# Queries rotated by VectorE from the raw projection, values projected in the odd slots, in a six-layer windowed transformer stage

## The chip, the cores and the metric

The kernel runs on one core of one Trainium2 chip, as one launch. The metric is the device time of that launch in microseconds. A program of many stages runs one after the other on the core's five engines: TensorE (matrix products and transposes), VectorE, ScalarE, GpSimd and SyncE, which only issues DMAs here.

## The reference, cut to what matters

The model is a chain of attention and feed-forward blocks on a tensor of 4 x 512 tokens with 128 features. The change is in one of them, `L2_ffn`, a transformer of six layers with 16 heads of 64 features and a window of 32 tokens:

```python
def attn_layer(x, Wqkv, qs, ksc, Wo):
    q, k, v = jnp.split(x @ Wqkv, 3, -1)          # heads of 64
    q = l2norm(q) * qs                            # q / max(|q|, 1e-12)
    k = l2norm(k) * ksc
    q = q * cos * scale + rotate_half(q) * sin * scale
    k = k * cos * inv + rotate_half(k) * sin * inv     # inv = 1 / scale
    out = local_attention(q, k, v)                # window 32, this block and the one before
    return out.transpose(0, 2, 1, 3).reshape(b, n, INNER) @ Wo

def ffn_layer(x, g, bln, W1, b1, W2, b2):
    hg = (layernorm(x) * g + bln) @ W1 + b1        # 2 x 341 columns
    a, gate = jnp.split(hg, 2, -1)
    return a * gelu(gate) @ W2 + b2

for i in range(6):
    x = attn_layer(shift_tokens(x), ...) + x
    x = ffn_layer(shift_tokens(x), ...) + x
```

The norm is one number for each token and head, so it can be multiplied in before or after the rotation.

## The kernel before

The stage is `transformer32` (line 780). The tokens are cut into 16 tiles of 128; the 16 heads into two groups of 8. A layer has thus 32 groups, and the six layers have 192, numbered n or G. The work is written by hand as a software pipeline over **slots**, one for each group (`slots()`): in slot s, group s is `now` (scores, softmax, weighing of the values), s+1 is `turn` (its rotated queries and keys are transposed), s+2 is `mid` (its keys are rotated), s+3 is `ahead` (projected, squared, summed, normalised, its queries rotated). A tile is finished every second slot. In even slots TensorE also mixes the heads of a tile (`mix_heads`) and makes the second feed-forward product of the tile before (`down`); in odd slots it makes the layer norm's transposes (`turn_sum`, `turn_norm`) and the first feed-forward product (`gate_up`), and ScalarE the Gelu, which wants another function table and back again (lines 1247 and 1253). An even and an odd slot together, a pair, are one tile of one layer.

Each engine does its part of every slot in a fixed written order and waits on semaphores for the others. What touches the change:

- `project` (line 1043, matmul on 1055) makes queries, keys and values of a group, each 128x512, into three PSUM banks `wa`. Before, all three of `ahead` are made in each slot. The values are copied into SBUF by ScalarE (`copy_v`, 1244), from where SyncE moves pieces of them by DMA into `vw` (`move`).
- ScalarE squares queries and keys (`square`, 1205); VectorE sums them by head (`sums`, 1299), limits them from below (`floor`, 1303); ScalarE makes inverse roots with a logarithm and an exponential (`roots`, 1217 and 1219); VectorE multiplies them into queries and keys (`normalise`, 1310), giving `qn`.
- GpSimd rotates (`rotate`): a product with the cosines into `ra` (999), two half-wide products with the sines into `rb` (1000, 1001), and their sum (1010 for keys, 1016 for queries).
- TensorE transposes the result (`turn_qk`, 1093), the softmax's numerators (`turn_p`, 1085) and the weighed output (`turn_o`, 1112). VectorE's `t_o` (1372) is the weighed output divided by its sums, and `t_ln` (1366) the normalised tile of the feed-forward part.
- VectorE's order in a slot: `add_heads` (1319, odd), scores' maximum and difference (1345, 1347), `gated` (1326, even), layer norm's statistics (odd), the queries' sums, `add_ffn` (1334, even), the keys' sums, the floor, `t_ln` (odd), `t_o`, and `normalise` of queries and keys.
- Of the feed-forward part's 341 columns the third chunk has 85, and its instructions work on 85 rows or columns (`HC`).

Of the kernel before, what the change touches and what calls it, by code (L numbers as in the profile page):

```python
# [20 lines left out]
P = 128  # L21
# [758 lines left out]
def transformer32(nc, g, dram, name, depth, heads, hid, wqkv, qs, ks, wo, ln_g, ln_b, w1, b1, w2, b2):  # L780
# [32 lines left out]

    wa_job, T_job, T_list = {}, {}, []
# [8 lines left out]

    with Stage(nc, name) as st:
        w_qkv = st.sb("w_qkv", [P, 2, 3 * INNER])
        w_o = st.sb("w_o", [P, 2, heads // 2, DIM])
        w_1 = st.sb("w_1", [P, 2, 2 * hid])
# [15 lines left out]
        ssq = st.sb("ssq", [P, 2, 16])  # L843
        logs = st.sb("logs", [P, 2, 16])
        inv = st.sb("inv", [P, 2, 16])
        qn = st.sb("qn", [P, 2, 8, HD])
# [30 lines left out]
        zeroed = st.sem("zeroed")  # L877
        resid_in = st.sem("resid_in")
# [13 lines left out]
        normed = st.event("normed", 2)  # L892
        q_rot = st.event("q_rot", 3)
        k_rot = st.event("k_rot", 3)
        q_roped = st.event("q_roped")
        k_roped = st.event("k_roped")
# [33 lines left out]
        with nc.Block() as block:  # L930
            @block.sync
            def _(sp):
                def load(l):
# [10 lines left out]
                    sp.dma_start(w_1[:, z, :], w1[l]).then_inc(sem, 16)  # L944
# [13 lines left out]

                load(0)
                sp.wait_ge(zeroed, 4)  # L960
# [25 lines left out]
            def _(pool):  # L986
                pool.memset(vn[:, :, :, :, :], 1.0).then_inc(zeroed, 1)
# [4 lines left out]
                def rotate(kind, n):  # L992
                    r, done = (0, q_rot) if kind == "q" else (1, k_rot)
                    t = tile_of(n)
                    cos, sin = rot[:, layer_of(t) % 2, 2 * r, t % TPB, :], rot[:, layer_of(t) % 2, 2 * r + 1, t % TPB, :]
                    pool.wait_ge(normed.sem, normed.at(n, r + 1))
                    if n >= 2:
                        pool.wait_ge(T_up.sem, T_up.at(T_job[kind, n - 2]))
                    pool.tensor_tensor(ra[:, n % 2, r], qn[:, r], spread(cos, 1, 8), ALU.mult).then_inc(done.sem, 1)  # L999
                    pool.tensor_tensor(rb[:, n % 2, r, :, 0:32], qn[:, r, :, 32:64], spread(sin[:, 0:32], 1, 8), ALU.mult).then_inc(done.sem, 1)  # L1000
                    pool.tensor_tensor(rb[:, n % 2, r, :, 32:64], qn[:, r, :, 0:32], spread(sin[:, 32:64], 1, 8), ALU.mult).then_inc(done.sem, 1)  # L1001

                for even, now, turn, mid, ahead, tail, ffn, last in slots():
# [3 lines left out]
                    if mid is not None:  # L1007
                        rotate("k", mid)
                        pool.wait_ge(k_rot.sem, k_rot.at(mid, 3))
                        pool.tensor_tensor(ra[:, mid % 2, 1], ra[:, mid % 2, 1], rb[:, mid % 2, 1], ALU.add).then_inc(k_roped.sem, 1)  # L1010
                    if ahead is not None:
                        if ahead % SLOTS == 0:
                            pool.wait_ge(tables.sem, tables.at(layer_of(tile_of(ahead)), 6))
# [2863 lines left out]
```

## Time and profile before

| | |
|---|---|
| median of 3 runs | 3893.35 us (3887.17 to 3898.36) |
| the profiled execution | 3903.03 us, its span 3901.3 us |
| mean granted TensorE clock | 0.958 |
| TensorE busy | 3535.7 us (91%) |
| VectorE busy | 2444.6 us (63%) |
| ScalarE busy | 2288.7 us (59%) |
| GpSimd busy | 2084.5 us (53%) |
| this stage | about 1457 to 3270 us |

The times are of one execution taken by the hardware profiler. Busy shares over the whole span mix stages with different limits, so the stage is read by itself: first how full each engine is in a quiet stretch, then who waits for whom, then the order of the work in one pair. In the names of the rows, `t_` stands for this stage's tiles; PE is TensorE, PEld its weight load, DVE VectorE, ACT ScalarE, POOL GpSimd, SPq the DMA issues of SyncE. The granted clock is 1.00 for 2.4 GHz and 0.50 for 1.2 GHz.

### The profile page before, as it was taken

What the parts mean: (1) busy time and instruction counts of PE and PEld (TensorE: products, weight loads), DVE (VectorE), ACT (ScalarE), POOL (GpSimd) and SP (SyncE); (2) the same over time, 40 slices, a digit from 0 to 9 for tenths busy, and PEclk for the clock granted to TensorE, in tenths of its full rate; (3) what the DMA queues carried; (4) which work ended last, traced back from release to release, by engine and by line L of the source; (5) the groups of instructions that cost most, each with busy time, mean ns of one, the idle gap of its engine ahead of it and who ended that gap; (6) DMA issues with size and microseconds to landing.
All of it is one profiled execution on the core that took longest, in us unless ns stands there. A gap on an engine that the chain in (4) does not pass through costs nothing. (4 is left out here: it accounts for less than half of the span.)

```text
span 3901.3 us, 124853 instructions
## 1 busy us (share of the span) xinstructions
PE 3535.7 (91%) x52653; PEld 2416.1 (62%) x52653; DVE 2444.6 (63%) x5150; ACT 2288.7 (59%) x4664; POOL 2084.5 (53%) x2227
## 2 busy tenths in 40 slices
PE   7996999998999988999999999999999996968885
PEld 4664555544566655766676666676676775846664
DVE  4446445512566646777777777677677775568885
ACT  2233555522455555766776676676676775457775
POOL 2003000000121128888888888888888884177773
PEclk9997999999899999999999999999999997989997
DMA  1000000010000003112112211211211111121010
GB/s 27 2 3 24 1 1 1 1 31 7 1 2 2 2 18 85 48 49 70 47 48 60 58 48 46 73 47 45 72 48 46 47 48 25 31 79 24 21 24 20
DMA packets 155562, 130.09 MB, mean 33 GB/s; under 512 B 53592, under 2 KB 144768, under 8 KB 154112
## 3 DMA queue, kind: packets, MB, share of 16 engines
q1 hardware_dynamic: 155008, 122.09, 12.0%
q8 instruction: 422, 6.91, 0.8%
q14 instruction: 132, 1.08, 0.1%
HBM read 31.93 MB, written 3.54 MB: 9 GB/s over the span
## 5 line engine op out<-in xcount | busy, mean ns | idle before, releaser
L1055 PE MATMUL t_wa<-t_w_qkv,t_resid 128*128 128x512 f32 x1152 | 606.6, 627 | 16.2 <-DMA t_scales<-in_L_ffn_k_scale 11.8
L999 POOL TENSOR_TENSOR t_ra<-t_qn,t_rot 128x512 f32<-128x512 f32 x384 | 490.1, 1276 | 179.3 <-DVE t_qn L1310 175.4
L1205 ACT ACTIVATE t_sq<-t_wa 128x512 f32<-128x512 f32 x384 | 227.6, 593 | 172.8 <-PE t_wa L1055 171.7
L3037 DVE TENSOR_REDUCE a_nmax<-a_A 128x2 f32<-128x1024 f32 (+3 forms) x256 | 206.1, 823 | 126.9 <-PE a_A L2935 124.6
L1345 DVE TENSOR_REDUCE t_nmax<-t_S 128x8 f32<-128x512 f32 x192 | 132.8, 692 | 238.1 <-PE t_S L1077 232.7
L1000 POOL TENSOR_TENSOR t_rb<-t_qn,t_rot 128x256 f32<-128x256 f32 x384 | 279.8, 729 | 0.0
L1001 POOL TENSOR_TENSOR t_rb<-t_qn,t_rot 128x256 f32<-128x256 f32 x384 | 279.6, 728 | 0.0
L3030 POOL TENSOR_SCALAR_AFFINE_SELECT a_pt<-a_pt 128x512 f32<-128x512 f32 x128 | 79.7, 634 | 371.9 <-ACT a_pt L3010 371.9
L1299 DVE TENSOR_REDUCE t_ssq<-t_sq 128x8 f32<-128x512 f32 x384 | 261.1, 683 | 17.9 <-ACT t_sq L1205 12.7
L1310 DVE SCALAR_TENSOR_TENSOR t_qn<-t_inv,t_wa 128x512 f32<-128x512 f32 x384 | 249.7, 680 | 13.0 <-POOL t_rb L1001 5.7
L1055 PEld LDWEIGHTS t_wa<-t_w_qkv,t_resid 128*128 128x128 f32 x1152 | 186.7, 195 | 113.9 <-issue 88.2
L1093 PEld LDWEIGHTS t_T<-ident,t_ra 128*128 128x128 f32 x1536 | 185.1, 143 | 115.7 <-issue 104.3
L1016 POOL TENSOR_TENSOR t_ra<-t_ra,t_rb 128x512 f32<-128x512 f32 x192 | 246.0, 1281 | 15.0
L1010 POOL TENSOR_TENSOR t_ra<-t_ra,t_rb 128x512 f32<-128x512 f32 x192 | 244.0, 1271 | 15.1
L3010 ACT ACTIVATE a_pt<-a_B 128x512 f32<-128x512 f32 (+1 forms) x384 | 176.5, 528 | 118.6 <-PE a_B L2946 118.6
L1093 PE MATMUL t_T<-ident,t_ra 128*128 128x128 f32 x1536 | 240.1, 279 | 0.7 <-ACT t_gg L1251 0.5
L2455 POOL COPY a_rep<-a_rden 128x512 f32<-128x512 f32 x32 | 19.6, 613 | 390.9 <-DVE a_rden L2484 390.9
L1123 PE MATMUL t_misc<-t_oT,t_w_o 128*128 128x128 f32 x1536 | 198.9, 283 | 0.9 <-DVE t_resid L1334 0.9
L1104 PEld LDWEIGHTS t_S<-t_vw,t_pT 64*32 64x32 f32 x9216 | 132.4, 106 | 91.9 <-issue 91.7
L1077 PE MATMUL t_S<-t_kT,t_qT 64*32 64x64 f32 x12288 | 169.5, 223 | 20.4 <-issue 20.4
L1123 PEld LDWEIGHTS t_misc<-t_oT,t_w_o 128*128 128x128 f32 x1536 | 180.6, 193 | 10.3 <-issue 1.4
L2946 PE MATMUL a_B<-a_Q,a_K 32*128 32x384 f32 (+3 forms) x1024 | 183.0, 453 | 1.0 <-ACT a_pt L3010 0.6
(498 smaller groups left out, 9340.0 us busy)
## 6 DMA issues: line engine op xcount, KB each, us to landing
t_vw<-t_vn SPq DMA_DIRECT2D x768, 66.0 KB
t_vw<-t_vn SPq DMA_DIRECT2D x672, 33.0 KB
t_w_qkv<-in_L_ffn_Wqkv SPq DMA_DIRECT2D x6, 1536.0 KB, 6.6
t_v<-t_vn SPq DMA_DIRECT2D x56, 132.0 KB, 2.8
t_vw<-t_nothing SPq DMA_DIRECT2D x96, 33.0 KB
t_w_o<-in_L_ffn_Wo SPq DMA_DIRECT2D x6, 512.0 KB
f_h<-t_L_ffn_h_w SPq DMA_DIRECT2D x2, 1024.0 KB, 7.5
t_w<-in_L_ffn_W SPq DMA_DIRECT2D x6, 341.0 KB
```

Source lines behind the costliest of these rows:

```text
L999: pool.tensor_tensor(ra[:, n % 2, r], qn[:, r], spread(cos, 1, 8), ALU.mult).then_inc(done.sem, 1)
L1000: pool.tensor_tensor(rb[:, n % 2, r, :, 0:32], qn[:, r, :, 32:64], spread(sin[:, 0:32], 1, 8), ALU.mult).then_inc(done.sem, 1)
L1001: pool.tensor_tensor(rb[:, n % 2, r, :, 32:64], qn[:, r, :, 0:32], spread(sin[:, 32:64], 1, 8), ALU.mult).then_inc(done.sem, 1)
L1010: pool.tensor_tensor(ra[:, mid % 2, 1], ra[:, mid % 2, 1], rb[:, mid % 2, 1], ALU.add).then_inc(k_roped.sem, 1)
L1016: pool.tensor_tensor(ra[:, ahead % 2, 0], ra[:, ahead % 2, 0], rb[:, ahead % 2, 0], ALU.add).then_inc(q_roped.sem, 1)
L1055: pe.matmul(bank, resid[:, b, lo:lo + P], w_qkv[:, l % 2, at:at + 512], start=True, stop=True).then_inc(wa_up.sem, 1)
L1093: m = pe.transpose(bank[:, j * P:(j + 1) * P], ra[:, n % 2, r, 2 * j:2 * j + 2, :].rearrange("p h d -> p (h d)"), ident[:, :])
L1123: m = pe.matmul(yT, w_o[:, l % 2, c, :], oT[:, c // 4, c % 4, :], start=(c == 0), stop=(c == 4 * NG - 1))
L1205: act.activation(sq[:, r].rearrange("p h d -> p (h d)"), wa[:, wa_job[kind, n] % 3, :], ACT.Square).then_inc(squared.sem, 1)
L1299: v.tensor_reduce(ssq[:, n % 2, 8 * r:8 * r + 8], sq[:, r], X, ALU.add).then_inc(summed.sem, 1)
L1310: v.scalar_tensor_tensor(out=qn[:, r], in0=spread(inv[:, n % 2, 8 * r:8 * r + 8], 2, HD), scalar=LIFT ** 0.5, in1=wa[:, wa_job[kind, n] % ...
L3037: v.tensor_reduce(nmax[:, u % 2, t, :].rearrange("p (j e) -> p j e", e=32)[:, 2 * pair:2 * pair + 2, 0], A[:, 2 * pair:2 * pair + 2, 0:(t ...
```

## The change

- **Queries.** VectorE no longer normalises them. From the raw projection in PSUM it makes the three rotary products itself (`rotate_queries`), placed behind `add_ffn` and ahead of the keys' sums. GpSimd adds them and then multiplies by the inverse roots. Keys are handled as before, in a tile `kn`.
- **Values' order.** TensorE projects no values in even slots. In odd slots it projects those of `mid`, where those of `ahead` used to be, and those of `ahead` between `turn_norm` and `turn_o`. ScalarE copies the first before the roots, and the second after the copy of the transposed output, ahead of the Gelus. The banks of `wa` are fixed by kind.
- **Floor.** The sums are written beside a constant 1e-24, and a maximum over the two replaces the comparison in place.
- **Padding.** The first and second feed-forward weights, the bias and the chunks are padded with zeros to 3 x 128; GpSimd clears the padding at the stage's start, and SyncE's first load of weights waits for all of GpSimd's clears.

```diff
-        for kind, n in (("q", ahead), ("k", ahead), ("v", ahead)):
+        for kind, n in [("q", ahead), ("k", ahead)] + [("v", n) for n in values(even, mid, ahead)]:
...
+                sp.wait_ge(zeroed, 7)
                 load(0)
-                sp.wait_ge(zeroed, 4)
...
+                pool.memset(w_1[:, :, :, hid:NH * P], 0.0).then_inc(zeroed, 1)
+                pool.memset(w_2[:, :, NH - 1, :], 0.0).then_inc(zeroed, 1)
+                pool.memset(b_1[:, :, :, NH - 1], 0.0).then_inc(zeroed, 1)
...
# GpSimd, queries
-                        rotate("q", ahead)
                         pool.wait_ge(q_rot.sem, q_rot.at(ahead, 3))
-                        pool.tensor_tensor(ra[:, ahead % 2, 0], ra[:, ahead % 2, 0], rb[:, ahead % 2, 0], ALU.add).then_inc(q_roped.sem, 1)
+                        pool.tensor_tensor(ra[:, ahead % 2, 0], ra[:, ahead % 2, 0], rb[:, ahead % 2, 0], ALU.add).then_inc(q_added.sem, 1)
+                        pool.wait_ge(q_added.sem, q_added.at(ahead))
+                        pool.wait_ge(inved.sem, inved.at(ahead))
+                        pool.tensor_tensor(ra[:, ahead % 2, 0], ra[:, ahead % 2, 0], spread(inv[:, ahead % 2, 0:8], 2, HD), ALU.mult).then_inc(q_roped.sem, 1)
...
# TensorE, even slots
                     if even:
-                        if ahead is not None:
-                            project("v", ahead)
                         if now is not None:
                             turn_p(now)
...
# TensorE, odd slots
-                        if ahead is not None:
-                            project("v", ahead)
+                        if mid is not None:
+                            project("v", mid)
...
                         if ffn is not None:
                             turn_norm(ffn)
+                        if ahead is not None:
+                            project("v", ahead)
                         if now is not None:
                             turn_o(now)
...
# ScalarE
+                    if not even and mid is not None:
+                        copy_v(mid)
                     if ahead is not None:
                         roots(ahead)
...
-                    if ahead is not None:
-                        copy_v(ahead)
                     if now is not None:
                         copy_o(now)
+                    if not even and ahead is not None:
+                        copy_v(ahead)
                     if ffn is not None:
                         gelus(ffn)
...
# VectorE
-                    v.tensor_scalar(ssq[:, n % 2, :], ssq[:, n % 2, :], 1e-24, None, ALU.max).then_inc(floored.sem, 1)
+                    v.tensor_reduce(floor_ssq[:, n % 2, :], ssq[:, n % 2, :, :], X, ALU.max).then_inc(floored.sem, 1)
...
+                def rotate_queries(n):
...
+                    v.wait_ge(wa_up.sem, wa_up.at(wa_job["q", n]))
...
+                    if n >= 2:
+                        v.wait_ge(T_up.sem, T_up.at(T_job["q", n - 2]))
+                    v.scalar_tensor_tensor(out=ra[:, n % 2, 0], in0=spread(cos, 1, 8), scalar=LIFT ** 0.5, in1=raw, op0=ALU.mult, op1=ALU.mult).then_inc(q_rot.sem, 1)
+                    v.scalar_tensor_tensor(out=rb[:, n % 2, 0, :, 0:32], in0=spread(sin[:, 0:32], 1, 8), scalar=LIFT ** 0.5, in1=raw[:, :, 32:64],
+                                           op0=ALU.mult, op1=ALU.mult).then_inc(q_rot.sem, 1)
+                    v.scalar_tensor_tensor(out=rb[:, n % 2, 0, :, 32:64], in0=spread(sin[:, 32:64], 1, 8), scalar=LIFT ** 0.5, in1=raw[:, :, 0:32],
+                                           op0=ALU.mult, op1=ALU.mult).then_inc(q_rot.sem, 1)
...
                     if last is not None:
                         add_ffn(last)
                     if ahead is not None:
+                        rotate_queries(ahead)
                         sums("k", ahead)
                         floor(ahead)
...
-                        normalise("q", ahead)
-                        normalise("k", ahead)
+                        normalise_keys(ahead)
```

## Rows read from the trace of the kernel before

**Rows 1.** Busy us by stretch: stretch, length, each engine's busy us (instructions), granted clock, DMA.
```profile
2500.00:2600.00 100.00, 98.12 (x1949) 70.87 (x1947) 74.05 (x164) 71.28 (x143) 88.25 (x95) 1.00 0.19 48
```

**Rows 2.** TensorE's waits in the stage, 1470 to 3260 us: total, times, longest.
```profile
PE t_T L1112 <- DVE t_o L1372: 38.0, 96, 1.0
```

**Rows 3.** Timeline of TensorE over one pair: start us, us, instruction.
```profile
2080.67 0.66 PE L1112 MATMUL t_T<-ident,t_o 128*128 128x128 f32 x4 [0.51 <-DVE t_o L1372]
...
2086.09 1.02 PE L1055 MATMUL t_wa<-t_w_qkv,t_resid 128*128 128x512 f32 x2
2086.95 0.60 PE L1085 MATMUL t_T<-ident,t_p 128*128 128x128 f32 x4
...
...
2091.27 0.60 PE L1112 MATMUL t_T<-ident,t_o 128*128 128x128 f32 x4
2091.80 0.30 PE L1070 MATMUL t_S<-t_mask,identb 64*32 64x256 bf16 x8
...
2097.91 0.28 PE L1133 MATMUL t_misc<-ident,t_ln 128*128 128x128 f32 x1
2098.71 0.66 PE L1112 MATMUL t_T<-ident,t_o 128*128 128x128 f32 x4 [0.51 <-DVE t_o L1372]
```

**Rows 4.** Timeline of ScalarE in the same pair.
```profile
2081.40 0.61 ACT L1240 ACTIVATE t_oT<-t_T 128x512 f32<-128x512 f32 x1
...
2086.00 0.62 ACT L1213 ACTIVATE t_p<-t_p 128x512 f32<-128x512 f32 x1
...
2090.48 0.58 ACT L1237 ACTIVATE t_kT<-t_T 128x512 f32<-128x512 f32 x1
2090.96 0.59 ACT L1244 ACTIVATE t_vn<-t_wa 128x512 f32<-128x512 f32 x1
```

**Rows 5.** Timeline of VectorE in the same pair.
```profile
2088.26 0.73 DVE L1334 SCALAR_TENSOR_TENSOR t_resid<-t_misc,t_b,t_resid 64x128 f32<-64x128 f32 x2 [1.44 <-PE t_misc L1149]
2089.02 0.69 DVE L1299 TENSOR_REDUCE t_ssq<-t_sq 128x8 f32<-128x512 f32 x1
2089.74 0.33 DVE L1303 TENSOR_SCALAR t_ssq<-t_ssq 128x16 f32<-128x16 f32 x1
...
2090.35 0.69 DVE L1372 TENSOR_TENSOR t_o<-t_S,t_rden 128x512 f32<-128x512 f32 x1
2090.96 1.28 DVE L1310 SCALAR_TENSOR_TENSOR t_qn<-t_inv,t_wa 128x512 f32<-128x512 f32 x2
...
2094.74 1.43 DVE L1299 TENSOR_REDUCE t_ssq<-t_sq 128x8 f32<-128x512 f32 x2
2096.21 1.29 DVE L1303 TENSOR_SCALAR t_ssq<-t_ssq 128x16 f32<-128x16 f32 x1
2097.42 0.40 DVE L1366 TENSOR_SCALAR t_ln<-t_misc,t_mv,t_rstd 128x128 f32<-128x128 f32 x1
...
2097.96 0.69 DVE L1372 TENSOR_TENSOR t_o<-t_S,t_rden 128x512 f32<-128x512 f32 x1
```

**Rows 6.** VectorE by instruction: two of `t_ssq`, ns min/median/max; then groups: busy us, mean ns.
```profile
L1299 DVE TENSOR_REDUCE t_ssq<-t_sq x384: 671/686/689, 1468.7 to 3242.0; 128x8 f32<-128x512 f32 x192
L1303 DVE TENSOR_SCALAR t_ssq<-t_ssq x192: 174/396/1316, 1471.0 to 3242.8; 128x16 f32<-128x16 f32 x192
...
L1303 DVE TENSOR_SCALAR t_ssq<-t_ssq 128x16 f32<-128x16 f32 x192 | 96.4, 502 | 6.7
L737 DVE TENSOR_TENSOR t_o<-t_S,t_rden 128x256 f32<-128x256 f32 x64 | 27.2, 425 | 2.2
```

**Rows 7.** Groups of GpSimd: busy us, mean ns, idle before.
```profile
L999 POOL TENSOR_TENSOR t_ra<-t_qn,t_rot 128x512 f32<-128x512 f32 x384 | 490.1, 1276 | 179.3 <-DVE t_qn L1310 175.4 <-issue 3.7
```

**Rows 8.** Weight loads of the 85-column chunk in the stage.
```profile
L1142 PEld LDWEIGHTS t_T<-t_lnT,t_w 128*85 128x85 f32 x376 | 49.8, 155 | 0.0
```

**Rows 9.** Timeline of the stage's head: first load issued, last clear.
```profile
1457.13 0.33 SPq L937 DMA_DIRECT2D t_w_qkv<-in_L_ffn_Wqkv  x1
...
1463.73 0.11 POOL L990 MEMSET t_resid<- 128x4 f32 x1
```

More of the change, by code:

```diff
@@ L811, in slots, with values @@
             yield s % 2 == 0, group(s), group(s + 1), group(s + 2), group(s + 3), part(s, 0), part(s, 1), part(s, 2)
+    def values(even, mid, ahead):
+        return [] if even else [n for n in (mid, ahead) if n is not None]
     wa_job, T_job, T_list = {}, {}, []
     for even, now, turn, mid, ahead, tail, ffn, last in slots():
-        for kind, n in (("q", ahead), ("k", ahead), ("v", ahead)):
+        for kind, n in [("q", ahead), ("k", ahead)] + [("v", n) for n in values(even, mid, ahead)]:
             if n is not None:
@@ L1139, in gate_up @@
                         bank = turn_bank(kind, t)
-                        for c, (at, size) in enumerate(HC):
-                            lo = half * hid + at
-                            m = pe.matmul(bank[0:size, c * P:(c + 1) * P], w_1[:, l % 2, lo:lo + size], lnT[:, :], start=True, stop=True)
+                        for c in range(NH):
+                            m = pe.matmul(bank[:, c * P:(c + 1) * P], w_1[:, l % 2, half, c * P:(c + 1) * P], lnT[:, :], start=True, stop=True)
                         m.then_inc(T_up.sem, 1)
@@ L1147, in down @@
                     pe.wait_ge(h_in.sem, h_in.at(t, NH))
-                    for c, (at, size) in enumerate(HC):
-                        m = pe.matmul(fT, w_2[0:size, l % 2, c, :], hT[0:size, c, :], start=(c == 0), stop=(c == NH - 1))
+                    for c in range(NH):
+                        m = pe.matmul(fT, w_2[:, l % 2, c, :], hT[:, c, :], start=(c == 0), stop=(c == NH - 1))
                     m.then_inc(f_up.sem, 1)
@@ L1249, in gelus @@
                     bank = turned("gate", t)
-                    for c, (at, size) in enumerate(HC):
-                        act.activation(gg[0:size, c, :], bank[0:size, c * P:(c + 1) * P], ACT.Gelu,
-                                       bias=b_1[0:size, l % 2, 1, c:c + 1]).then_inc(gelu_in.sem, 1)
+                    for c in range(NH):
+                        act.activation(gg[:, c, :], bank[:, c * P:(c + 1) * P], ACT.Gelu, bias=b_1[:, l % 2, 1, c:c + 1]).then_inc(gelu_in.sem, 1)
                     act.preload_act_table_set("natural_log_exp_and_others")
@@ L1323, in gated @@
                     v.wait_ge(T_up.sem, T_up.at(j))
[L1324 removed]
+                    for c in range(NH):
                         v.wait_ge(gelu_in.sem, gelu_in.at(t, c + 1))
[L1326 to L1327 removed]
+                        v.scalar_tensor_tensor(out=hT[:, c, :], in0=T[:, j % 2, c * P:(c + 1) * P], scalar=b_1[:, l % 2, 0, c:c + 1],
+                                               in1=gg[:, c, :], op0=ALU.add, op1=ALU.mult).then_inc(h_in.sem, 1)
                 def add_ffn(t):
```

71 lines of the change are left out of this document (40 added, 31 removed).

## The prediction

> **What bounds the kernel now.** I first looked for the stage that the change touches: lines 930 to 1374, the six-layer windowed transformer, which takes about 1800 of the 3901 us. Then I asked, stretch by stretch, which engine is full there. A quiet stretch of 100 us shows TensorE busy 98.12 us at a granted clock of 1.00 (its 2.4 GHz level), GpSimd 88.25, VectorE 74.05 and ScalarE 71.28 [rows 1]. A busy TensorE can still be a waiting one, so the waits come next: in the whole stage TensorE's one frequent wait is for VectorE's `t_o` ahead of the transpose on L1112, 96 times and 38.0 us together [rows 2], once in each pair of slots. The timeline of one pair then gives the order. One odd slot's `turn_o` starts at 2080.67, the next at 2098.71 [rows 3]: a pair, that is one tile of one layer, takes 18.04 us. There are 96 tiles; I count 95 full pairs.
>
> I measure the pair from X, the start of `turn_o` in the odd slot. TensorE reaches `turn_p` of the even slot at X+6.28 (2086.95) and its `turn_o` at X+10.60 (2091.27); the odd slot's scores start at Y = 2091.80 = X+11.13, and the next `turn_o` comes at Y+6.91 after its wait of 0.51 [rows 3]. Everything but that 0.51 us is TensorE's own queue. So taking work off GpSimd is worth nothing by itself: it is busy 88%, and what counts is what the change does to the two chains that end in TensorE's waits, and these run through ScalarE and VectorE, which are only some 70% busy but stand in a fixed order.
>
> **ScalarE, even slot.** Before the change ScalarE copies `oT` at 2081.40, loads the Gelu table, runs the Gelus, loads the table back, squares, and ends the exponentials at 2086.00 + 0.62 = 2086.62, X+5.95 [rows 4]. TensorE doesn't feel that, since the values' projection (2086.09 to 2086.95, 0.86 us [rows 3]) stands between. The change takes that projection out of the even slot, and it puts `copy_v(ahead)` between the copy of `oT` and the first table load. Two copies start 0.48 us apart (2090.48 and 2090.96 [rows 4]); I take 0.50. The exponentials then end at X+6.45, and with 0.06 for the hand-over (`t_o` ends at 2098.65, its transpose starts at 2098.71 [rows 3, 5]) `turn_p` starts at X+6.51, 0.23 later than before, with TensorE idle for about 1.1 us ahead of it, where it used to project.
>
> **VectorE, even slot.** From `turn_p` to the start of `add_ffn` there are 2088.26 - 2086.95 = 1.31 us, and from there to the keys' sums 0.76 [rows 3, 5]. New `add_ffn` begins at X+7.82 and VectorE is free of it at X+8.58. Here the change inserts the queries' three products, ahead of the keys' sums, the floor and `t_o`. The trace has no such instruction; by form the nearest are the 128x512 scalar_tensor_tensor of L1310, two of which take 1.28 us, so 0.60 from start to start [rows 5], and a 128x256 tensor_tensor from PSUM, 425 ns [rows 6], or about 0.35 from start to start. Together 0.60 + 0.36 + 0.36, about 1.33 us. Bounds: 0.68, as if they cost one 512-wide instruction, and 0.68 + 2 x 0.425 = 1.53 with no overlap. I take 1.33, the sum of the nearest rows. The normalising of the queries that goes (0.60) stood after `t_o`, where nothing waited for it, so it pays for none of this.
>
> Then follow the keys' sums (0.72 until the floor starts), the floor, 0.28 with the reciprocal until `t_o` starts, and `t_o` (0.69) [rows 5]. The floor is a 16-element tensor_scalar that took 0.33 here and between 174 and 1316 ns in all, median 396; the tensor_reduce on L1299, 32 times as large, took between 671 and 689 [rows 5, 6]. The new floor is such a reduce, and I give it the 0.17 us of the undisturbed tensor_scalar, with 0.50 as the other end (mean of the old one: 96.4 us in 192). The Trainium skill bears on this (SBUF — State Buffer, "Who interferes with whom"): an fp32 tensor_scalar in SBUF can take the port pair that GpSimd also uses and is then blocked by it, and a tensor_reduce on this chip never is. By that rule the floor would take 0.17; were the reduce to wait as the old one did, the sum would be 2 x 0.33 x 95 = 63 us more. So `t_o` ends at X + 8.58 + 1.33 + 0.72 + 0.17 + 0.28 + 0.69 = X+11.77, and `turn_o` starts at X+11.83 instead of X+10.60. TensorE is there long before: `down`, the keys' transposes, `weigh` and `mix_heads` take the 4.32 us after `turn_p` that they take now (2086.95 to 2091.27 [rows 3]), so it arrives at X+10.83 and is idle for 1.0 us a second time. **The even slot is 1.23 us later.**
>
> Another rule of the skill speaks against the split (VectorE: DVE Perf Modes, "The DRAIN you can't avoid"): a following operation does not start before the pipe is empty, so what counts is the number of operations. By it the three would cost 1.53, and both slots together 2 x 0.20 x 95 = 38 us more than my sum. The two on L1310 overlap, 1.28 for two of 0.68, so I stay with 1.33.
>
> **VectorE and TensorE, odd slot.** Old: the queries' sums start at Y+2.94 (2094.74), the floor at Y+4.41 and it takes 1.29 us waiting for GpSimd, `t_ln` starts at Y+5.62 and takes 0.40, `t_o` starts at Y+6.16 [rows 5]. New: queries' sums 2.94, products 3.59, keys' sums 4.92, floor 5.64, `t_ln` 5.85 to 6.25 (0.04 behind the floor), `t_o` 0.54 after `t_ln`'s start as now, 6.39 to 7.08. The 1.33 us of products are thus mostly paid by the floor's 1.1 us. TensorE was ready for `turn_norm` at Y+6.11 (2097.91) [rows 3] and now gets to it at Y+6.31; then 0.28 for it, 0.86 for the values' projection that now stands there, and `turn_o` at Y+7.45, with `t_o` ready. **The odd slot is 0.54 us longer**: the old wait of 0.51 is filled, but by 0.86 us that came from the other slot, and `turn_norm` is 0.20 late.
>
> **What is hidden.** GpSimd loses a 1.28 us product and two halves and gets one product back in each group [rows 7]; its added wait for the roots has the next slot's key products queued behind it, and a query is transposed two slots after it is made, so both are covered at nothing; without that cover it would be the rotated keys that come late, by the roots' 0.5 us. The SP queue gets the values of odd groups nearly a slot later, but still two slots before they are weighed; nothing. Padding to 128 rows: TensorE streams the same columns, and only the weight load of the third chunk grows. It takes 155 ns for 85 columns [rows 8]; in proportion it would be 233, 376 x 78 ns = 29 us at most if none of it were hidden; it is loaded beside the matmul ahead of it, so I take 0.
>
> **At the head, once.** The first weight load was issued at 1457.13 and now waits for all of GpSimd's clears, the last of which ends at 1463.84 [rows 9], plus three new small ones, which I put at 0.2 each from their size beside the 0.11 of that row. That is 7.3 us, on the path, as the first projection waits for these weights. The bounds are 6.7 and 8.
>
> **The sum.** (1.23 + 0.54) x 95 = 168 us, and 7: 175 us. The profiled execution took 3903 us, so that one would become 4078. The median of the runs is 3893, 10 us lower, and the same 175 on it gives **4068 us**. The bounds: products 0.68 to 1.53 and floor 0.17 to 0.50 move a pair by -1.0 (where TensorE's own queue takes over) to +1.0 us.
>
> **Rivals.**
> 1. *VectorE is covered, ScalarE isn't.* If the products fell into VectorE's own waiting time, only the late `turn_p` and the moved projection would count: `turn_o` at X+10.83, odd slot 6.11 + 0.28 + 0.86 = 7.25, so 0.23 + 0.34 more, a pair of 18.61. 0.57 x 95 + 7 = 61: 3954 us. For it: VectorE waits 1.44 us for TensorE ahead of `add_ffn` [rows 5]. Against it: the products stand behind that wait in VectorE's queue, not ahead of it.
> 2. *The other side: TensorE stays full.* The moved projection fills the 0.51 us wait and nothing else appears, so a pair takes 17.53: -48 + 7 = -41, 3852 us. It decides if `turn_p` can start by X+5.4, when TensorE now begins the projection that goes (2086.09). For it: TensorE is the full engine and the wait is real. Against it: even today the exponentials end at X+5.95.
> 3. *Worse than my sum.* The floor still waits for GpSimd (+63), or the new idle times bring TensorE's clock to its 1.2 GHz level for stretches. 4131 us by the first. Against the second: the clock is 1.00 in this stretch, and the idle times of 1.1 us are a tenth of a slot.
> 4. *No change* within measurement: only by a cancelling of these.
>
> **Chances.** My forecast 0.62, with a range of its own of 4015 to 4115; rival 1 0.14; rival 2 0.08; rival 3 0.13; rival 4 0.03. The range for 8 in 10 is 3950 to 4130: it takes in rival 1 and leaves out rival 2 and most of rival 3. About 0.3%, 12 us, is what a measurement can tell here. Faster: rival 2 and a little, 0.09; same 0.03; slower 0.88.
>
> **What would show it.** In the timeline of a quiet pair after the change: from `turn_o` to `turn_o` 19.8 us; L1085's transposes waiting about 1.1 us for the exponentials; the even slot's L1112 waiting about 1 us for `t_o`; the three products 1.33 us and always behind `add_ffn`; the floor near 0.17 with no spread; GpSimd's share of a quiet stretch well under 75%. I am wrong if TensorE still shows 98 us of 100, or if `turn_p` in the even slot has no wait.

## The result, and the profile after

The changed kernel takes **3982.71 us** (median of 4 runs, 3977.29 to 3984.95) against 3890.86 us before: ratio 1.0232, 95% interval 1.0212 to 1.0251. It is slower, as forecast, but by 92 us instead of 175. The profiled execution took 3981.91 us (span 3980.2), the one of before 3903. These two differ by 79 us, since that one of before lay 12 us above its median; the traces are compared with the 79.

Busy time in the same kind of quiet stretch after the change, columns as in [rows 1]:

```profile
2500.00:2600.00 100.00, 92.14 (x1846) 66.34 (x1844) 72.08 (x173) 65.84 (x131) 65.25 (x66) 1.00 0.18 44
```

GpSimd falls from 88.25 to 65.25 us of 100, and TensorE falls with it, from 98.12 to 92.14: the kernel bought room on an engine that held nothing up. TensorE's waits in the stage (total us, times, longest), to be read beside [rows 2]:

```profile
PE t_T L1102 <- ACT t_p L1229: 92.2, 101, 1.9
PE t_T L1129 <- DVE t_o L1406: 62.5, 96, 1.0
```

One wait was there before, of 38.0 us; now there are two, of 154.7 us together. TensorE's timeline over one pair, where the old one is [rows 3] (L1129 is `turn_o`, L1102 `turn_p`, L1150 `turn_norm`):

```profile
2200.94 0.60 PE L1129 MATMUL t_T<-ident,t_o 128*128 128x128 f32 x4
...
2207.34 0.66 PE L1102 MATMUL t_T<-ident,t_p 128*128 128x128 f32 x4 [0.94 <-ACT t_p L1229]
...
2212.54 0.66 PE L1129 MATMUL t_T<-ident,t_o 128*128 128x128 f32 x4 [0.65 <-DVE t_o L1406]
2213.12 0.30 PE L1087 MATMUL t_S<-t_mask,identb 64*32 64x256 bf16 x8
...
2219.31 0.33 PE L1150 MATMUL t_misc<-ident,t_ln 128*128 128x128 f32 x1
2219.48 1.02 PE L1072 MATMUL t_wa<-t_w_qkv,t_resid 128*128 128x512 f32 x2
2220.34 0.60 PE L1129 MATMUL t_T<-ident,t_o 128*128 128x128 f32 x4
```

The pair is 2220.34 - 2200.94 = 19.40 us, 1.36 more than 18.04. ScalarE in the same pair shows why `turn_p` is late: the added copy of the values (L1260) stands ahead of the table load, and everything behind it to the exponentials (L1229) moves with it.

```profile
2201.58 0.60 ACT L1256 ACTIVATE t_oT<-t_T 128x512 f32<-128x512 f32 x1 [0.63 <-PE t_T L1129]
2202.07 0.59 ACT L1260 ACTIVATE t_vn<-t_wa 128x512 f32<-128x512 f32 x1
2202.68 1.28 ACT L1263 ACT_TABLE_LOAD   x1
...
2206.67 0.62 ACT L1229 ACTIVATE t_p<-t_p 128x512 f32<-128x512 f32 x1
```

VectorE shows why `t_o` is late. The three products (L1333 to L1336) stand between `add_ffn` (L1367) and the keys' sums, the floor and `t_o`; compare [rows 5]:

```profile
2208.71 0.73 DVE L1367 SCALAR_TENSOR_TENSOR t_resid<-t_misc,t_b,t_resid 64x128 f32<-64x128 f32 x2 [1.22 <-PE t_misc L1165]
2209.48 0.69 DVE L1333 SCALAR_TENSOR_TENSOR t_ra<-t_rot,t_wa 128x512 f32<-128x512 f32 x1
2210.08 0.41 DVE L1334 SCALAR_TENSOR_TENSOR t_rb<-t_rot,t_wa 128x256 f32<-128x256 f32 x1
2210.41 0.41 DVE L1336 SCALAR_TENSOR_TENSOR t_rb<-t_rot,t_wa 128x256 f32<-128x256 f32 x1
2210.74 0.68 DVE L1318 TENSOR_REDUCE t_ssq<-t_sq 128x8 f32<-128x512 f32 x1
2211.46 0.19 DVE L1322 TENSOR_REDUCE t_floor_ssq<-t_ssq 128x16 f32<-128x32 f32 x1
...
2211.79 0.69 DVE L1406 TENSOR_TENSOR t_o<-t_S,t_rden 128x512 f32<-128x512 f32 x1
```

**Not every pair grew.** I took the start of `turn_o` in every odd slot and the 95 differences, for both traces. Together they went from 1769.1 to 1841.2 us, +72.1. The head of the stage, up to the first of these starts, added 2.8 us. The other 4 us lie outside the pairs, nearly all of them outside the stage: it begins 0.9 us earlier, and what stands behind it takes 5.2 us more (610.3 before, 615.5 after). But two pairs of each of the first five layers were long before and are nearly ordinary now (us per pair, layers 1 to 5):

```
                                       before                            after
the next layer's weights arrive        23.23 24.84 24.22 24.07 24.60     19.71 19.28 20.55 19.28 19.28
the next layer's first tables          23.32 23.32 23.57 24.20 23.36     20.45 20.45 20.45 20.45 20.45
```

These ten pairs went from 238.7 to 200.3 us, a gain of 38.4 us; the other 85 cost 72.1 + 38.4 = 110.5 us, 1.30 each. So the change loses more per ordinary pair than the total shows, and wins something back that my prediction never looked at. What the ten pairs were waiting for is read from the kernel before. At the weights, TensorE stops in the middle of a run of matmuls that wait for nothing:

```profile
2145.91 0.67 PE L1077 MATMUL t_S<-t_kT,t_qT 64*32 64x64 f32 x44
2149.99 0.64 PE L1077 MATMUL t_S<-t_kT,t_qT 64*32 64x64 f32 x20 [3.41 <-issue]
```

The busy times of that stop (columns as in [rows 1]) show the DMA engines 98% busy while the next layer's weights are loaded, and the granted clock on its way down; behind the stop it is at 0.50, the 1.2 GHz level, for 6.7 us:

```profile
2146.60:2150.00 3.40, 0.01 (x3) 0.01 (x3) 0.26 (x1) 0.00 (x0) 3.10 (x4) 0.79 0.98 284
2148.70:2155.40 6.70, 5.42 (x30) 2.96 (x30) 2.79 (x7) 1.72 (x3) 2.82 (x3) 0.50 0.47 115
```

There are five such stops before, 3.3 to 4.9 us each; the longest after is 1.0 us. The DMA view of the stop shows what TensorE lacked. Its queues are (packets, MB, share of the engines):

```profile
q1 hardware_dynamic: 1820, 0.95, 96.1%
q8 instruction: 1, 0.02, 1.8%
```

Queue q8 brings instructions, and over the whole launch it is

```profile
q8 instruction: 422, 6.91, 0.8%
```

TensorE has 108,040 records in this trace (matmuls, weight loads and its waits), 256 for each of the 422 packets, so q8 is taken to be TensorE's own queue. The one packet in the stop starts at 2147.67, takes 0.96 us, and TensorE runs again 1.36 us after it. It comes 12.0 us behind the packet before it, where the median in the stage is 6.65. The other stops look the same. Over the kernel before, e1, e7, e8 and e10 below there are 22 stops of more than 3 us: in each of them one q8 packet starts inside the stop, 10.8 to 14.7 us behind its predecessor, and TensorE runs again 1.2 to 1.6 us after it has landed. And the five stops of the kernel before lie 11,519 to 11,521 TensorE records apart, which is 45 times 256. So TensorE stops at the border of a block of instructions that the busy DMA engines bring late.

At a layer's first slot, `make_tables` is long before the change and short after it. By instruction, ns min/median/max, first the kernel before:

```profile
L1292 DVE TENSOR_TENSOR t_rot<-t_base,t_scales x12: 287/807/1348, 1467.6 to 2954.6; 128x128 f32<-128x128 f32 x12
```

and the kernel after:

```profile
L1311 DVE TENSOR_TENSOR t_rot<-t_base,t_scales x12: 277/279/285, 1474.2 to 3010.3; 128x128 f32<-128x128 f32 x12
```

The six products of one layer took 4.4 us before (2051.13 to 2055.52) and 1.75 after. Before, GpSimd's own products run beside the long ones, and where GpSimd rests an instruction of the same shape is short:

```profile
2051.93 0.90 POOL L1000 TENSOR_TENSOR t_rb<-t_qn,t_rot 128x256 f32<-128x256 f32 x1
2052.18 0.81 DVE L1292 TENSOR_TENSOR t_rot<-t_base,t_scales 128x128 f32<-128x128 f32 x1
2053.64 1.52 POOL L1016 TENSOR_TENSOR t_ra<-t_ra,t_rb 128x512 f32<-128x512 f32 x1
2053.97 1.34 DVE L1292 TENSOR_TENSOR t_rot<-t_base,t_scales 128x128 f32<-128x128 f32 x1
2055.24 0.28 DVE L1293 TENSOR_TENSOR t_rot<-t_base,t_scales 128x128 f32<-128x128 f32 x1
```

After the change no GpSimd instruction runs beside any L1311: GpSimd waits there for VectorE. Before, TensorE waited for what stands behind the tables:

```profile
2056.10 0.33 PE L1129 MATMUL t_misc<-ident,t_resid 128*128 128x128 f32 x1 [3.33 <-DVE t_resid L1319]
```

### The profile page after: what moved, and what is told of

Read it like the earlier page. It is cut to its first block and busy times, and to the rows that moved or that the text cites. A ratio compares the mean times of both kernels' runs of the same rounds, so it can differ in the third digit from the quotient of the medians.

```text
span 3980.2 us, 124966 instructions
## 1 busy us (share of the span) xinstructions
PE 3531.9 (89%) x52643; PEld 2412.7 (61%) x52653; DVE 2475.7 (62%) x5535; ACT 2289.3 (58%) x4664; POOL 1779.3 (45%) x1846
## 5 line engine op out<-in xcount | busy, mean ns | idle before, releaser
L1072 PE MATMUL t_wa<-t_w_qkv,t_resid 128*128 128x512 f32 x1152 | 591.0, 613 | 22.1 <-DMA t_scales<-in_L_ffn_k_scale 19.3
L1027 POOL TENSOR_TENSOR t_ra<-t_ra,t_rb 128x512 f32<-128x512 f32 x192 | 243.6, 1269 | 305.6 <-DVE t_rb L1336 305.6
L1013 POOL TENSOR_TENSOR t_ra<-t_kn,t_rot 128x512 f32<-128x512 f32 x192 | 244.5, 1274 | 0.0
L1233 ACT ACTIVATE t_logs<-t_floor_ssq 128x16 f32<-128x16 f32 x192 | 41.4, 216 | 304.2 <-DVE t_floor_ssq L1322 304.1
L1030 POOL TENSOR_TENSOR t_ra<-t_ra,t_inv 128x512 f32<-128x512 f32 x192 | 200.5, 1044 | 18.1 <-POOL t_ra L1027 0.4
L1102 PE MATMUL t_T<-ident,t_p 128*128 128x128 f32 x768 | 124.1, 284 | 92.2 <-ACT t_p L1229 92.2
L1020 POOL TENSOR_TENSOR t_rstd<-t_vare,half 128x1 f32<-128x1 f32 x96 | 52.9, 551 | 317.6 <-DVE t_vare L1389 317.6
L1256 ACT ACTIVATE t_oT<-t_T 128x512 f32<-128x512 f32 x192 | 114.8, 598 | 126.3 <-PE t_T L1129 126.3
```

The lines of the kernel that those rows point to most:

```text
L1013: pool.tensor_tensor(ra[:, n % 2, 1], kn[:, :], spread(cos, 1, 8), ALU.mult).then_inc(k_rot.sem, 1)
L1027: pool.tensor_tensor(ra[:, ahead % 2, 0], ra[:, ahead % 2, 0], rb[:, ahead % 2, 0], ALU.add).then_inc(q_added.sem, 1)
L1030: pool.tensor_tensor(ra[:, ahead % 2, 0], ra[:, ahead % 2, 0], spread(inv[:, ahead % 2, 0:8], 2, HD), ALU.mult).then_inc(q_roped.sem, 1)
L1072: pe.matmul(bank, resid[:, b, lo:lo + P], w_qkv[:, l % 2, at:at + 512], start=True, stop=True).then_inc(wa_up.sem, 1)
```

## The experiments

Eleven kernels. The kernel before ran beside them at 3891.7 to 3893.0 us, and their ratios are to those runs; the changed kernel's is to the 3890.86 us above. "Pair" is the ordinary pair of the trace, from one odd slot's `turn_o` to the next (18.04 before, 19.40 after). The code under each heading is the part of the edit that matters; `...` marks what is left out.

```
                                          median us   ratio to before [95%]       pair us
after                                     3982.71     1.0232 [1.0212, 1.0251]     19.40
e1  after, queries on GpSimd again        3927.14     1.0082 [1.0056, 1.0108]     18.24
e2  after, values' order as before        3948.54     1.0135 [1.0106, 1.0163]     18.97
e3  after, products ahead of add_ffn      3897.65     1.0006 [0.9992, 1.002]      18.45
e4  after, copy_v a slot later            3937.44     1.0103 [1.0072, 1.0134]     18.90
e5  e3 and e4                             3854.99     0.9898 [0.9884, 0.9913]     17.93
e6  before, one more wait on TensorE      3874.14     0.9952 [0.9937, 0.9967]     18.04
e7  before, floor as a reduce             3890.96     0.9992 [0.9982, 1.0001]     17.9
e8  e5, exponentials first, short head    3891.99     0.9996 [0.9986, 1.0005]     18.2
e9  before, weights a slot later          3878.09     0.9962 [0.9947, 0.9977]     18.0
e10 before, tables spread over slots      3869.22     0.995  [0.9935, 0.9965]     18.0
e11 e5, tables spread, short head         3845.60     0.9884 [0.9868, 0.9901]     17.93
```

**e1: the queries' products back on GpSimd.**

```diff
+                def normalise_queries(n):     # VectorE, behind t_o, as before
...
-                        rotate_queries(ahead)                    # VectorE
+                        rotate_q(ahead)                          # GpSimd, three products and the sum
```

> The changed kernel with the queries normalised by VectorE and rotated by GpSimd again; padding, floor and the values' order stay. A quiet pair of the changed kernel takes 19.40 us, of the kernel before 18.04. Theory A (two chains: VectorE's products hold t_o in the even slot, ScalarE's copy of the values holds the exponentials): the wait of 0.65 us ahead of the even slot's turn_o goes, that of 0.94 ahead of turn_p stays, the odd slot is some 0.1 shorter; a pair of 18.65, 3915 us if the long pairs at the layers' starts and loads stay as in the changed kernel, about 3960 if they come back with GpSimd's load (there were ten or so of 23 to 25 us before, and none over 21 after). Rival B (the values' order does all of it): the pair stays at 19.4 and the time at 3983. Rival C (the products do all of it): the pair is back at 18.0.

Measured: 3927.14 us, a pair of 18.24. TensorE's waits in the stage:

```profile
PE t_T L1112 <- ACT t_p L1239: 88.1, 98, 1.9
...
PE t_S L1104 <- issue: 17.0, 7, 4.2
PE t_misc L1156 <- DVE t_resid L1355: 16.4, 6, 3.2
```

The wait for `t_o` has gone (2.0 us in 3 times) and the one for `t_p` stays: the first is the products' doing, the second is not. The products cost 19.40 - 18.24 = 1.16 us of a pair. The other two rows are the long pairs: nine of the ten are back, at 22.3 to 25.2 us, and only the first at the weights is not (18.8). So both kinds depend on this edit and not on the values' order. The tables' products beside the busier GpSimd, by instruction, are as long as in the kernel before:

```profile
L1321 DVE TENSOR_TENSOR t_rot<-t_base,t_scales x12: 285/808/1346, 1473.6 to 2972.5; 128x128 f32<-128x128 f32 x12
```

**e2: the values' order as before.**

```diff
     def values(even, mid, ahead):
-        return [] if even else [n for n in (mid, ahead) if n is not None]
+        return [n for n in (ahead,) if n is not None]
...
                     if even:
+                        if ahead is not None:
+                            project("v", ahead)
...
```

> The changed kernel with the values projected and copied where the kernel before has them, in every slot; the products stay on VectorE. Theory A: turn_p starts without a wait as it did before the change, t_o in the even slot is as late behind it as now (5.2 us), so a pair of about 18.95 and 3943 us. Rival B (the order does it): pair 18.0, 3891 or less. Rival C (the products do it): 19.4.

Measured: 3948.54 us, a pair of 18.97. The projection stands ahead of `turn_p` again. TensorE now waits for `t_o` 189 times, 110.3 us, in nearly every slot instead of every second one: the products are late for `t_o` in both slots, which the 0.86 us of projection covered in the odd one. The values' order costs 0.43 us of a pair on top of the products (19.40 - 18.97). Without them it is 0.20 (e1's 18.24 - 18.04), with the new floor and the padding counted in, which e1 keeps.

**e3: the same products, ahead of `add_ffn`.**

```diff
                     if ahead is not None:
                         sums("q", ahead)
+                    if ahead is not None:
+                        rotate_queries(ahead)
                     if last is not None:
                         add_ffn(last)
                     if ahead is not None:
-                        rotate_queries(ahead)
                         sums("k", ahead)
```

> The changed kernel with the three products ahead of add_ffn instead of behind it. VectorE waits 1.22 us there for TensorE in the even slot. Theory A: the products fall into that wait, t_o ends near X+10.4 while TensorE arrives at X+10.95, the even slot's wait of 0.65 goes, a pair of 18.75 and 3925 us; turn_p still waits 0.94. If the products cost because VectorE has too much work rather than because of their place: no change, 19.4.

Measured: 3897.65 us over 10 runs, no different from before, a pair of 18.45. The work is the same and the wait for `t_o` is gone. VectorE's timeline:

```profile
2213.11 0.68 DVE L1333 SCALAR_TENSOR_TENSOR t_ra<-t_rot,t_wa 128x512 f32<-128x512 f32 x1
2213.70 0.41 DVE L1334 SCALAR_TENSOR_TENSOR t_rb<-t_rot,t_wa 128x256 f32<-128x256 f32 x1
2214.03 0.42 DVE L1336 SCALAR_TENSOR_TENSOR t_rb<-t_rot,t_wa 128x256 f32<-128x256 f32 x1
2214.41 0.73 DVE L1367 SCALAR_TENSOR_TENSOR t_resid<-t_misc,t_b,t_resid 64x128 f32<-64x128 f32 x2
```

`add_ffn` used to start behind 1.22 us of idle; there is no bracket on it now. The products run in the time in which VectorE waited for TensorE's L1165 (`down`). TensorE's `turn_o` has no wait:

```profile
2206.64 0.60 PE L1129 MATMUL t_T<-ident,t_o 128*128 128x128 f32 x4
...
2213.05 0.66 PE L1102 MATMUL t_T<-ident,t_p 128*128 128x128 f32 x4 [0.94 <-ACT t_p L1229]
...
2217.42 0.60 PE L1129 MATMUL t_T<-ident,t_o 128*128 128x128 f32 x4
```

With X at 2206.64, `turn_o` comes at X+10.78. This is rival 1 of the prediction, which said X+10.83 and a pair of 18.61; it comes about by moving one line.

**e4: the values of `ahead` copied in the next slot.**

```diff
-                    if not even and mid is not None:
+                    if mid is not None:
                         copy_v(mid)
...
-                    if not even and ahead is not None:
-                        copy_v(ahead)
                     if ffn is not None:
                         gelus(ffn)
```

> The changed kernel with ScalarE's copy of ahead's values moved from in front of the Gelus into the next, even slot, behind the copy of pT, where ScalarE waits 2.9 us for the floor. Theory A: the exponentials of the even slot end 0.6 us earlier, turn_p waits 0.35 instead of 0.94 and everything behind it follows, so a pair of 18.8 and 3929 us. If TensorE's wait ahead of turn_p is made good behind it by the wait for t_o (that is, if the time is VectorE's own), nothing changes: 19.4.

Measured: 3937.44 us, a pair of 18.90. The wait for `t_p` halves, from 92.2 to 46.1 us; the one for `t_o` stays at 62.6. The copy is worth 0.50 us of a pair, its full time from start to start.

**e5: both moves.**

> Both moves in one kernel: products ahead of add_ffn, and the copy of ahead's values in the next even slot. Alone they took a pair from 19.40 to 18.45 and 18.88. Theory A (two chains in a row, each with its own wait): they add up, 19.40 - 0.95 - 0.52 = 17.95 a pair, 3850 us. If one chain only hid the other: no shorter than 18.4, 3897.

Measured: 3854.99 us, 1.0% faster than before, a pair of 17.93. The two moves gave 0.95 and 0.50 alone and 1.47 together: they were two separate terms. TensorE's waits:

```profile
PE t_T L1102 <- ACT t_p L1229: 45.6, 101, 1.9
...
PE t_T L1129 <- DVE t_o L1405: 2.0, 3, 1.0
```

So the change's parts are good for something, but not in the places where it put them.

**e6: the kernel before, with one more wait on TensorE.** The changed kernel's projection of the queries waits for two events, the old one for one. I added a second to the old one, on an event that is always past by then.

```diff
                         else:
+                            if kind == "q":
+                                pe.wait_ge(squared.sem, squared.at(n - 1, 1))
                             pe.wait_ge(normed.sem, normed.at(n - 1, 1 if kind == "q" else 2))
```

> The kernel before with one wait more on TensorE ahead of each projection of queries, for the squares of the group before, which are always there by then. In the kernel before TensorE stops for 3.3 to 4.9 us in the middle of the scores' matmuls once in each of five layers, with nothing awaited, while the next layer's weights are moved; the matmuls left to run then are 41 (of two groups), 28, 20, 12, 4, eight fewer in each layer. The changed kernel has this second wait and no such stop. Theory D (the stop comes at a fixed place of TensorE's instruction stream, where new instructions have to be fetched, and the additional instruction moves that place off the time of the weight load): the stops go or move to other lines, about 25 us less, 3867 us. Rival E (the stop goes because of the changed kernel's slower slots or its order of the DMAs): nothing changes, 3892 us, stops at the same counts.

Measured: 3874.14 us, 0.5% faster for an added wait. The pairs at the weights take 18.7 to 19.1 us instead of 23.2 to 24.8; those at a layer's start keep their 23.2 to 24.4. TensorE's stops with nothing to wait for are this row of its waits in the kernel before:

```profile
PE t_S L1077 <- issue: 20.4, 6, 4.9
```

and the last of these in e6, beside the unchanged wait at a layer's start:

```profile
PE t_misc L1131 <- DVE t_resid L1321: 17.9, 7, 3.4
...
PE t_S L1079 <- issue: 3.9, 5, 1.3
```

The instruction packets at the weights are still late here, up to 11.6 us behind their predecessors, but TensorE stands still for 1.4 us at most. The added instruction moves where the borders of the blocks fall in its program.

**e7: the kernel before, with the new floor.**

```diff
-                    v.tensor_scalar(ssq[:, n % 2, :], ssq[:, n % 2, :], 1e-24, None, ALU.max).then_inc(floored.sem, 1)
+                    v.tensor_reduce(floor_ssq[:, n % 2, :], ssq[:, n % 2, :, :], X, ALU.max).then_inc(floored.sem, 1)
...
```

> The kernel before with the floor as a maximum over pairs, alone. Theory F: the floor takes 0.19 us in place of a mean of 0.50, t_ln is 1.1 us earlier in the odd slot, where TensorE does not need it, and t_o 0.15 earlier, where it does: a pair of 17.9, 3879 us. If weigh decides when t_o can start and not the floor: 18.04, no change. The long pairs at the layers' starts stay, since make_tables still shares VectorE's time with a busy GpSimd.

Measured: 3890.96 us over 10 runs, ratio 0.9992, no difference. The pairs at the weights (22.3 to 25.2) and at a layer's start (22.7 to 24.1) stay long. Alone, the floor is worth 0 to 0.2 us of a pair (17.86 to 18.0), and the spread that it takes away was mostly absorbed.

**e8: e5, with the exponentials ahead of the queries' square in even slots, and the first weight load behind the three small clears only.**

```diff
-                sp.wait_ge(zeroed, 7)
+                sp.wait_ge(zeroed, 3)
                 load(0)
+                sp.wait_ge(zeroed, 7)
...
+                    if even and now is not None:
+                        exponentials(now)
                     if ahead is not None:
                         square("q", ahead)
-                    if now is not None:
+                    if not even and now is not None:
                         exponentials(now)
```

> e5 with ScalarE's exponentials ahead of the squares of the queries in even slots, and the first weight load waiting only for the padding's clears. Theory A: the exponentials end another 0.5 us earlier, turn_p has no wait left, and TensorE's own queue sets the pair at about 17.55; the head is 6 us shorter; 3893 - 47 for the pairs - 45 for the long pairs that are gone = about 3805 us. If something else holds TensorE in the even slot: 17.9 and 3845.

Measured: 3891.99 us, 37 us slower than e5. The pair goes up to 18.2. `turn_p` has no wait any more, but the squares of the queries come later, and with them the products and `add_ffn`, and the heads' mixing (L1141) now waits for `add_ffn`'s result in nearly every second slot; `t_o` is no longer what TensorE waits for (1.5 us in 2 times):

```profile
PE t_misc L1141 <- DVE t_resid L1368: 20.7, 93, 0.2
```

The weighing is later as well: it starts 1.9 us behind `turn_p` instead of 1.7, as ScalarE comes to copy `turn_p`'s result only behind the squares. And TensorE's stops at the weights return, although this kernel has the second wait of e6:

```profile
2146.96 0.94 PE L1095 MATMUL t_S<-t_kT,t_qT 64*32 64x64 f32 x45 [3.56 <-issue]
```

There are five of them, of 3.3 to 4.4 us, at the same places of TensorE's program as in the kernel before (within a record of one another).

**e9: the kernel before, with the next layer's weights one slot later.**

```diff
-                    if G % SLOTS == 8 and layer_of(t) + 1 < depth:
+                    if G % SLOTS == 9 and layer_of(t) + 1 < depth:
```

> The kernel before with the next layer's weights loaded one slot later, and TensorE's instructions as they were. In e8 TensorE had the second wait and stopped again (3.3 to 4.4 us, in the scores' matmuls of the loads), so the number of waits alone doesn't decide. Theory G (the stop is a coincidence in time: TensorE reaches a place where it needs new instructions while the load keeps the DMA engines busy): with the load 9 us later the place is passed before the load begins, the five pairs of 23.6 to 24.9 us are gone or much shorter, some 25 us less, 3867 us. Rival H (the load stops TensorE wherever it comes): five stops of the same length a slot later, 3893 us.

Measured: 3878.09 us (0.9962). The pairs at the weights, one later now, fall to 18.2 to 20.5 us, those at a layer's start stay at 22.3 to 24.5. The same bytes at another moment stop TensorE for 2.1 us at most.

**e10: the kernel before, with the tables made ahead.** One of the six products in each of six even slots of the layer before, instead of all six at the head of a layer's first slot.

```diff
-                    if ahead is not None and ahead % SLOTS == 0:
-                        make_tables(layer_of(tile_of(ahead)))
+                    if ahead is not None and 20 <= ahead % SLOTS < 32 and even and layer_of(tile_of(ahead)) + 1 < depth:
+                        make_table(layer_of(tile_of(ahead)) + 1, (ahead % SLOTS - 20) // 2)
```

> The kernel before with the six products of the rotary tables of a layer made one by one in the even slots of the layer before, in place of all six in a row at its start. Theory I (at a layer's start VectorE's products with two SBUF inputs wait for GpSimd's, 4.4 us for six against 1.6 at the head, TensorE then waits 3.4 us for the residual and its clock falls): the five pairs of 23.3 to 23.6 us at the layers' starts become 18.1, 5 x 5.3 = 26 us less, 3866 us. If these pairs are long for another reason of a new layer, the weights say: no change.

Measured: 3869.22 us (0.995). The pairs at a layer's start take 17.8 to 18.2 us, those at the weights keep 23.3 to 24.9 but for the first, 19.2. The two kinds of long pair are thus two causes, and each can be taken away alone.

**e11: e5, with the tables of e10 and the short head of e8.**

> e5 (products ahead of add_ffn, copy in the next even slot) with the tables spread as in e10 and the first weight load waiting for the padding's clears alone. From e5's 3855: the head 6 to 7 us less; the five first pairs of a layer 18.70 to 17.95, 4 us less; 3844 us. If a table's product lengthens VectorE's chain in its slot, six slots in each layer give back up to 0.4 us each, 12 us, and there is no gain over e5.

Measured: **3845.60 us** (3841.48 to 3849.43), 0.9884 of before [0.9868, 0.9901], the fastest of all: 45 us below the kernel before, 137 below the changed one. Pairs at a layer's start take 17.96 to 18.02 but for the last, 18.77; at the weights 18.7 to 19.4. What TensorE still waits for is the exponentials, 43.7 us in the stage.

## Why the prediction was right in direction and too high in size

By the profiled execution I said 4078 us and it took 3981.9, 96 us less. Step by step:

- **TensorE's queue as the measure, GpSimd's relief worth nothing: right for an ordinary pair.** GpSimd lost 23 points and TensorE gained none. Wrong at a layer's start, below.
- **ScalarE, even slot: right.** The exponentials end at X+6.35 (said 6.45), `turn_p` starts at X+6.40 (6.51) after a wait of 0.94 us (1.1). e4 takes this term alone and gets 0.50.
- **VectorE, even slot: right in kind, 0.18 us too large.** `add_ffn` at X+7.77 (said 7.82); products 1.26 us (1.33); the floor 0.19 us without a spread (0.17); `t_o` ends at X+11.54 (11.77) and `turn_o` starts at X+11.60 (11.83). Part of it is carried over from the exponentials. The even slot is 2213.12 - 2200.94 = 12.18 us, 1.05 more than 11.13, where I said 1.23.
- **Odd slot: +0.31 instead of +0.54.** `turn_norm` came at Y+6.19 instead of Y+6.31. I started `t_ln` 0.04 us behind the end of the floor; it starts 0.10 after the floor's start. Then the projection started 0.17 us behind `turn_norm`'s start and not 0.28. The pair is +1.36 for +1.77, and over the 85 ordinary pairs that is 150 us said, 110.5 measured: 40 of the 96 us.
- **The products' price.** The prediction set a rule of the Trainium skill against the split (VectorE: DVE Perf Modes, "The DRAIN you can't avoid"); it would add up full durations, 0.69 + 0.41 + 0.41 = 1.51 us. The same section says that a next operation that is not held back starts earlier, which the prediction left out. The trace has 1.26 from the first start to the next instruction's, so here the operations overlap.
- **The floor.** It took 185 to 189 ns in all 192 cases (said 0.17 us), where the tensor_scalar took 174 to 1316. The rule of the skill that I drew on (SBUF — State Buffer, "Who interferes with whom") agrees.
- **Head: right where it begins, 4.5 us too large where it ends.** The first weight load is issued behind the clears at 1463.42, and the first square starts 18.4 us after the stage's start instead of 10.9, 7.5 later for 7.3 said. But the first odd `turn_o` comes only 2.8 us later: from the first square to there it takes 32.8 to 33.2 us in the six kernels with the queries on GpSimd, and 28.3 to 30.4 in the seven with the products on VectorE. The prediction took the whole delay to be on the path. That its 7 us for everything but the pairs still came out (2.8 at the head, -0.3 at the tail, 4.3 outside the stage) is luck. The 5.2 us more behind the stage come in all seven kernels with the products on VectorE (615.5 to 616.8 us, against 608.8 to 612.0 in the other six), in code that the change does not touch; no run shows why.
- **Padding: not measured by itself.** No run takes it alone. The weight loads of a chunk now take 194 ns on average, where the short third chunk took 155, and TensorE has no wait for them.
- **The step that failed: "(1.23 + 0.54) x 95".** It takes all 95 pairs as alike. I had counted the pairs but read only one. Ten were 5 to 7 us longer than the rest, which the starts of [rows 3]'s L1112 over the whole stage would have shown, and the change takes most of that away. For these ten I said +18 and they gave -38: 56 of the 96 us. Here GpSimd's relief, which I had put at nothing, was worth something after all: 15.5 us at the layers' starts, where VectorE's table products had run beside GpSimd's work. The other 23 us come at the weights, where TensorE no longer stops for its instructions.

Rival 2, a full TensorE with 17.53 us a pair, did not come; its deciding point, `turn_p` at X+5.4, was missed by 1.0 us (X+6.40 measured). Rival 3's floor didn't wait, and the granted clock stayed at 1.00 from 1480 to 3340 us, where before it had fallen to 0.50 for 3 to 7 us at each long pair. The 3983 us lie below the forecast's own range (4015 to 4115) and within the wide one.

What the runs settle: the two terms of an ordinary pair (e3, e4, e5), the independence of the two kinds of long pair (e6, e9, e10), and that both come with the queries' products on GpSimd (e1) or, for the weights, with what else sets the moment (e6, e9). TensorE stops at the weights because its next block of instructions lands late: that is shown by the q8 packet inside each stop, by the steady 1.2 to 1.6 us from its landing to the next matmul, and by stops a whole number of 256-record blocks apart. That the packet is late because the weights fill the DMA engines rests on the busy share of 0.98 and on e9, where the same bytes at another moment leave at most 2.1 us. What stays open is when exactly a block border costs time: in the changed kernel a packet comes 12.6 us behind its predecessor and TensorE loses only 1.0 us, and e6 and e8 have the same second wait and opposite outcomes. The place of the border against the load decides, and no run gives a rule for it.

## What to carry to other kernels

Before multiplying a pair by its count, list the length of every pair: the outliers are a second bottleneck with its own causes, and a change can win there what it loses elsewhere. Work moved onto an engine in a fixed order costs what stands behind it in that order, so look for the instruction with an idle bracket in front and put the new work there: one moved line was worth 85 us here (e3), another 45 (e4). A high busy share alone does not make an engine worth relieving: GpSimd, busy for 88 of 100 us, held up no ordinary pair, while work put on VectorE (74) and ScalarE (71) did. And when an engine stops without waiting for anything, look at the instruction queues in the DMA view.

## What the runs showed of the hardware

- TensorE can stop for 3.3 to 4.9 us within a run of matmuls that wait for nothing, while a load of the next layer's weights fills the DMA engines (busy share 0.98). In each of 22 such stops one packet of the instruction queue q8 (0.02 MB, one for each 256 records of TensorE) starts 10.8 to 14.7 us behind its predecessor, against a median of 6.65, and TensorE goes on 1.2 to 1.6 us after it has landed. The granted clock is 0.50 for 3 to 7 us from about the end of the stop. An added wait that is always met (e6) or a load 9 us later (e9) took away 19 and 14 us over five layers; e8's reordering brought the stops back.
- A VectorE product of two fp32 inputs in SBUF, 128x128, takes 277 to 285 ns where no GpSimd instruction runs beside it (all 12 cases after the change), about 807 ns beside GpSimd's products L1000 and L1001, and 1343 to 1348 ns beside its addition L1016. GpSimd's instructions are longer there too: 0.90 us against the mean of 0.73 for L1000, and 1.52 against 1.28 for L1016. The Trainium skill says that such an instruction contends with GpSimd for SBUF (SBUF — State Buffer, "Who interferes with whom"); the trace agrees. The queries' products, with one input in PSUM, took 675 to 690 ns for 128x512 in all 192 cases of e8.
- GpSimd's 128x512 product with the roots, spread over 64 columns each, took 1044 ns against 1269 to 1274 for its other 128x512 instructions.
